# Decoder layer on one core: causal masks and results of the attention spread over other engines

## The reference

```python
x = layernorm(x + linear_attention(x))          # 16 heads of 64, relu features
x = layernorm(x + xattn(x, ctx))                # below
x = layernorm(x + ffn(x))                       # 8 experts, each row goes to one

# xattn: 16 heads of 16
att  = einsum('bhqd,bhkd->bhqk', q, k) * scale
att  = where(causal, att, -inf)
y    = einsum('bhqk,bhkd->bhqd', softmax(att), v)
attc = einsum('bhqd,bhkd->bhqk', qc, kc) * scale    # 1024 context rows, no mask
y    = y + einsum('bhqk,bhkd->bhqd', softmax(attc), vc)
return y @ Wp + bp
```

## Time and profile before

| what | value |
|---|---|
| median of 3 runs | 2330.27 us (2329.63 to 2338.28) |
| the profiled execution | 2329.88 us |
| its span | 2328.1 us |
| granted TensorE clock, mean | 0.993 |
| TensorE busy | 96% |
| VectorE busy | 60% |
| ScalarE busy | 45% |
| POOL busy | 13% |
| mean DMA rate | 101 GB/s |

### The profile page before, as it was taken

One profiled execution on the slowest core, in us unless ns is written; L12 is line 12 of the kernel. 1 busy time (PEld: TensorE's weight loads), 2 busy tenths in 40 slices (PEclk: granted clock), 3 DMA queues, 4 the chain that ended last, 5 costly groups with the idle time before them and its releaser, 6 DMA issues. The chain is left out here.

```text
span 2328.1 us, 52307 instructions
## 1 busy us (share of the span) xinstructions
PE 2229.4 (96%) x17506; PEld 1405.5 (60%) x17507; DVE 1401.9 (60%) x3568; ACT 1046.8 (45%) x1432; POOL 309.6 (13%) x516
## 2 busy tenths in 40 slices
PE   8999999999999999999999999999999999799998
PEld 4556555656465556555565656564655565499997
DVE  2578357844785458735883478447854686245554
ACT  1256524652466226632564256524662366233332
POOL 1010011101100110011010111011001101122222
PEclk9999999999999999999999999999999999899999
DMA  7440035102510162005300350026102520655553
GB/s 236 161 152 24 1 114 187 47 2 83 203 61 2 48 229 70 2 11 195 118 24 4 131 179 35 1 83 217 47 2 77 201 69 2 210 175 183 183 181 107
DMA packets 116585, 236.20 MB, mean 101 GB/s; under 512 B 19790, under 2 KB 43471, under 8 KB 114160
## 3 DMA queue, kind: packets, MB, share of 16 engines
q1 hardware_dynamic: 112928, 224.56, 28.8%
q0 software_dynamic: 3408, 8.41, 1.0%
HBM read 154.37 MB, written 73.17 MB: 98 GB/s over the span
## 5 line engine op out<-in xcount | busy, mean ns | idle before, releaser
L1152 ACT ACTIVATE es<-ps 128x1024 f32<-128x1024 f32 (+1 forms) x704 | 659.7, 983 | 306.7 <-PE ps L764 250.3
L1350 DVE TENSOR_REDUCE craw<-ps 128x1 f32<-128x512 f32 x1024 | 641.0, 683 | 131.8 <-PE ps L727 120.4
L727 PE MATMUL ps<-hk,hq 64*128 64x512 f32 x1024 | 279.2, 464 | 19.9 <-DVE craw L1350 12.0
L792 PE MATMUL ps<-es,vca 128*17 128x256 f32 x4096 | 276.7, 382 | 1.2 <-ACT es L1152 1.1
L1347 DVE TENSOR_REDUCE craw<-ps 128x1 f32<-128x512 f32 (+3 forms) x512 | 219.5, 484 | 75.8 <-PE ps L723 72.0
L762 PE MATMUL ps<-hq,hk 64*128 64x512 f32 x1024 | 235.5, 428 | 1.6 <-ACT es L1152 1.6
L727 PEld LDWEIGHTS ps<-hk,hq 64*128 64x128 f32 x1024 | 130.3, 184 | 176.6 <-DVE craw L1350 114.0
L632 POOL TENSOR_SCALAR_AFFINE_SELECT es<-es 128x256 f32<-128x256 f32 x256 | 99.4, 406 | 991.7 <-ACT es L1152 990.9
L764 PE MATMUL ps<-mrow,minus 64*128 64x512 f32 x1024 | 215.5, 391 | 0.0
L1661 ACT ACTIVATE hT<-ph,b1s 128x128 f32<-128x128 f32 x312 | 88.9, 368 | 183.9 <-PE ph L1624 183.9
L792 PEld LDWEIGHTS ps<-es,vca 128*17 128x17 f32 x4096 | 93.9, 96 | 115.1 <-issue 62.4
(11 more groups left out here) (206 smaller groups left out, 2812.4 us busy)
## 6 DMA issues: line engine op xcount, KB each, us to landing
w1s<-in_w1T SPq DMA_DIRECT2D x39, 1024.0 KB, 5.3
hk<-scr_kc SPq DMA_DIRECT2D x64, 512.0 KB, 5.2
scr_kc<-staged SPq DMA_DIRECT2D x16, 1024.0 KB, 4.3
scr_qc<-staged SPq DMA_DIRECT2D x32, 512.0 KB, 4.6
scr_q<-staged SPq DMA_DIRECT2D x32, 512.0 KB, 5.1
hq<-scr_qc SPq DMA_DIRECT2D x56, 256.0 KB, 5.0
hq<-scr_q SPq DMA_DIRECT2D x56, 256.0 KB, 4.2
hk<-scr_k SPq DMA_DIRECT2D x56, 256.0 KB, 5.2
```

The costliest lines, as they stand in the source:

```text
L727: last = mm(pb, hq[i][at, T + t * P:T + (t + 1) * P], hk[i][at, T + half * BANK:T + (half + 1) * BANK], start=True, stop=True)
L792: last = mm(z[row:row + VW, (2 - len(tiles)) * P:2 * P], (va if own else vca)[:, j, p * HB + a, :], weights, start=n in (0, NSELF), stop=n ...
L1152: nc.scalar.activation(es[:, k % ERING, :].rearrange("p (a c) -> p a c", a=HB)[:, :, 0:w], eslot[k % 2][:].rearrange("p (a c) -> p a c", a ...
L1350: last = v.reduce_max(craw[p % 2][:, t, a:a + 1, half], pb, AX.X)
```

## The change

- The two mask matmuls of each self tile go. VectorE takes the masked maximum in one operation, `tensor_tensor_reduce`: it adds `causal` (bf16, in SBUF, zeros with the mask as its last 128 columns) to the scores in PSUM, writes the sum back to the same place, and gives the maximum of each row. A semaphore increment on nothing (`s_held`) stands between the wait and this operation.
- `mpad` holds the maxima of all four query tiles in one 128x128 block, written by one operation. TensorE turns it with one transpose. ScalarE spreads it over `mrow` with four copies of 128 columns, each scaled by a column of `inblock` that is one on the partitions of its tile and zero elsewhere; `minus` has ones in more places to match.
- For the first seven pairs ScalarE copies the turned sums to `zt` in SBUF (`turned`), VectorE takes only the reciprocal, two maxima later in its order (DVE_ORDER, LATER), and POOL multiplies and adds (`results`). The bank of a turned result is freed by ScalarE. The last pair stays with VectorE.
- In the setup 12 DMAs become one (LOADS is 31, was 42). SP waits for the sums of the last pair ahead of the experts' weights.

```diff
+def reciprocals_later():
+    order = [e for e in ORDER if e[0] in ("max", "turn")]
+    for p in range(PAIRS - 1):
+        at = order.index(("turn", p, 0))
+        order.insert(min(at + 1 + LATER, order.index(("turn", p + 1, 0))), order[at])
+        del order[at]
+    return order
...
+        mpad = sb("mpad", [P, P])
+        zt = sb("zt", [P, 2 * NT * HB, VW])
...
             sp.wait_ge(s_av, NEXP * (nb + 1))
+            sp.wait_ge(s_ys, PAIRS * (nb + 1))
...
+                def results(p):
+                    pool.wait_ge(s_rec, b * (PAIRS - 1) + (p + 1))
+                    pool.sem_inc(s_past, 1)
+                    nc.gpsimd.tensor_tensor(yn[:], zt[:, :, 0:XD], rec[:].unsqueeze(2).broadcast_to([P, 2 * NT * HB, XD]),
+                                            ALU.mult).then_inc(s_yn, 1)
+                    pool.wait_ge(s_yn, b * (PAIRS - 1) + (p + 1))
+                    pool.sem_inc(s_past, 1)
+                    rows = sums_of()
+                    nc.gpsimd.tensor_tensor(y_s[:, :, p * HB * XD:(p + 1) * HB * XD], rows[:, 0], rows[:, 1],
+                                            ALU.add).then_inc(s_ys, 1)
...
                     if kind == "row":
                         pe.wait_ge(s_mrow, cur(b, PAIRS, p + 1))
+                    elif kind == "turn" and former != LAST_TURN:
+                        pe.wait_ge(s_zt, cur(b, PAIRS - 1, p + 1))
...
-                        mm(pb[:, col:col + w], hq[i][at, t * P:(t + 1) * P], hk[i][at, 0:w], start=True, stop=False)
-                        for half in range(2):
-                            last = mm(pb[:, col + w - P:col + w], iden2[at, half, :], mqk2[at, half, :],
-                                      start=False, stop=half == 1)
+                        last = mm(pb[:, col:col + w], hq[i][at, t * P:(t + 1) * P], hk[i][at, 0:w], start=True, stop=True)
...
-                for t in range(NT):
-                    last = tr(pb[:, t * P:(t + 1) * P], mpad[:, t, :], ident[:])
-                last.then_inc(s_ring, 1)
+                tr(pb[:, 0:P], mpad[:], ident[:]).then_inc(s_ring, 1)
...
-                    nc.scalar.activation(mrow[p % 2][:], mbank[n % MBANKS], ACT.Copy).then_inc(s_mrow, 1)
+                    for t in range(NT):
+                        last = nc.scalar.activation(mrow[p % 2][:, t * P:(t + 1) * P], mbank[n % MBANKS][:, 0:P],
+                                                    ACT.Copy, scale=inblock[:, t:t + 1])
+                    last.then_inc(s_mrow, 1)
...
+                def turned(p):
+                    s = RING_AT["turn", p, 0]
+                    act.wait_ge(s_ring, cur(b, NRING, s + 1))
+                    act.wait_ge(s_ys, cur(b, PAIRS, p))
+                    tv = mbank[s % MBANKS].rearrange("p (n d) -> p n d", d=ZW)
+                    nc.scalar.activation(zt[:], tv[:, :, 0:VW], ACT.Copy).then_inc(s_zt, 1)
...
                     if n >= 2 * NT:
+                        dve.sem_inc(s_held, 1)
                         for t, col in MAX_SELF[n - 2 * NT]:
-                            last = v.reduce_max(craw[p % 2][:, t, a:a + 1, 2], pb[:, col:col + (t + 1) * P], AX.X)
+                            own = pb[:, col:col + (t + 1) * P]
+                            last = v.tensor_tensor_reduce(own, own, causal[:, (NT - 1 - t) * P:NT * P], 1.0, LOWEST,
+                                                          ALU.add, ALU.max, craw[p % 2][:, t, a:a + 1, 0])
...
-                        v.tensor_copy(rows[:, :, :, 0], raw[2])
-                        v.tensor_tensor(rows[:, :, :, 1], raw[0], raw[1], ALU.max).then_inc(s_max, 1)
+                        rows = mpad[:].rearrange("p (a t c) -> p t a c", a=HB, t=NT)
+                        v.tensor_tensor(rows[:, :, :, 0:2], craw[p % 2][:, :, :, 0:2], craw[p % 2][:, :, :, 0:3:2],
+                                        ALU.max).then_inc(s_max, 1)
+
+                def reciprocals(p):
+
+                    dve.wait_ge(s_zt, cur(b, PAIRS - 1, p + 1))
+                    v.reciprocal(rec[:], zt[:, :, XD]).then_inc(s_rec, 1)
```

More of the change, by code:

```diff
@@ L39 @@
 NEG = -1e30
+LOWEST = -3.0e38
 HROW = 4 * XD
+MROW = HROW // NT
 ZW = 32
@@ L102 @@
 BEHIND = 4
+LATER = 2
 SWAP = (0, 1)
@@ L165 @@
 ORDER = heads_order()
+def reciprocals_later():
[5 more added lines that the diff above has]
+    return order
+DVE_ORDER = reciprocals_later()
 RING = [e for e in ORDER if e[0] in ("max", "row", "turn")]
 RING_AT = {e: n for n, e in enumerate(RING)}
-NRING, NRED = len(RING), sum(e[0] != "row" for e in RING)
-RED_AT = {e: sum(f[0] != "row" for f in RING[:n + 1]) for n, e in enumerate(RING)}
+NRING, NRED = len(RING), sum(e[0] == "max" for e in RING) + 1
+LAST_TURN = ("turn", PAIRS - 1, 0)
+RED_AT = {e: sum(f[0] == "max" or f == LAST_TURN for f in RING[:n + 1]) for n, e in enumerate(RING)}
 NEXP = PAIRS * NU
@@ L435, in _ @@
             const(number[:], number_d)
-            for n, src in enumerate((ident_d, mask_qk, mask_kq)):
-                for half in range(2):
-                    for at in range(2):
-                        const(cstage[at * HROW:(at + 1) * HROW, n, half, :], src[half * HROW:(half + 1) * HROW])
+            const(r_s[:, 0, 0:P], mask_qk)
             const(wvl[:], wv_l.rearrange("(k p) r -> p k r", p=P))
@@ L623, in _, with cut @@
                                             stage[:, stg, 0, at:at + T].bitcast(F32), ALU.subtract).then_inc(s_low, 1)
[L625 to L634, removed]
+                def cut(p, n):
+                    k = p * NU + n
+                    pool.wait_ge(s_exp, cur(b, NEXP, k + 1))
+                    pool.sem_inc(s_past, 1)
+                    for j, col in EXP_SELF[n]:
+                        block = es[:, k % ERING, :].rearrange("p (a c) -> p a c", a=HB)[:, :, col:col + P]
+                        last = nc.gpsimd.affine_select(block, block, [[0, HB], [1, P]], ALU.is_ge, 0.0, base=0,
+                                                       channel_multiplier=-1)
+                    last.then_inc(s_cut, 1)
+                def results(p):
[4 more added lines that the diff above has]
+                    pool.wait_ge(s_yn, b * (PAIRS - 1) + (p + 1))
+                    pool.sem_inc(s_past, 1)
+                    rows = sums_of()
+                    nc.gpsimd.tensor_tensor(y_s[:, :, p * HB * XD:(p + 1) * HB * XD], rows[:, 0], rows[:, 1],
+                                            ALU.add).then_inc(s_ys, 1)
+                for kind, p, n in ORDER:
+                    if kind == "exp" and n < NSELF:
+                        cut(p, n)
+                    elif kind == "turn" and p < PAIRS - 1:
+                        results(p)
                 pool.wait_ge(s_act, cur(b, N_ACT, ACT_AT["kf1"]))
@@ L1165, in _ @@
                         maxima_rows(p)
+                    elif kind == "turn" and p < PAIRS - 1:
+                        turned(p)
                     elif kind == "exp":
@@ L1355, in reduce, with last_results @@
                             dve.wait_ge(s_ring, cur(b, NRING, RING_AT["row", p - 1, 0] + 1))
-                        raw = [craw[p % 2][:, :, :, w] for w in range(3)]
-                        rows = mpad[:].rearrange("p t (a c) -> p t a c", a=HB)
-                        v.tensor_copy(rows[:, :, :, 0], raw[2])
-                        v.tensor_tensor(rows[:, :, :, 1], raw[0], raw[1], ALU.max).then_inc(s_max, 1)
-                def results(p):
+                        rows = mpad[:].rearrange("p (a t c) -> p t a c", a=HB, t=NT)
[4 more added lines that the diff above has]
+                    v.reciprocal(rec[:], zt[:, :, XD]).then_inc(s_rec, 1)
+                def last_results():
+                    p = PAIRS - 1
                     s = RING_AT["turn", p, 0]
+                    dve.wait_ge(s_ys, cur(b, PAIRS, p))
                     dve.wait_ge(s_ring, cur(b, NRING, s + 1))
@@ L1369, in results @@
                     dve.wait_ge(s_red, cur(b, NRED, RED_AT["turn", p, 0]))
-                    rows = yn[:].rearrange("p (w t a) d -> p w t (a d)", w=2, t=NT)
+                    rows = sums_of()
                     v.tensor_tensor(y_s[:, :, p * HB * XD:(p + 1) * HB * XD], rows[:, 0], rows[:, 1], ALU.add).then_inc(s_ys, 1)
                     dve.wait_ge(s_ys, cur(b, PAIRS, p + 1))
-                for kind, p, n in ORDER:
+                for kind, p, n in DVE_ORDER:
                     if kind == "max":
                         reduce(p, n)
+                    elif kind == "turn" and p == PAIRS - 1:
+                        last_results()
                     elif kind == "turn":
-                        results(p)
+                        reciprocals(p)
                 dve.wait_ge(s_xb, cur(b, 2, 2))
```

32 lines of the change are left out of this document (19 added, 13 removed).

## The result

The changed kernel takes 2303.03 us (median of 4 runs, 2301.82 to 2304.03) against 2329.95 us before on the same chip: a ratio of 0.9878, 95% interval [0.9866, 0.989]. The forecast was 2304.0. The profiled execution took 2301.82 us, its span is 2299.9, and its mean granted clock is 0.989 where before it was 0.993. That last number is the first hint that the agreement hides something.

A forecast was written before the change was run, and what follows sets the result against it. The prediction took TensorE and VectorE, both nearly full and joined by three banks of scores, as the bound; 3.2 us a sequence times 8 gave 26 us, and 2329.9 - 26 = 2304 us, range 2263 to 2348.

The forecast's parts named there:

- the walk: Step-by-step timing of TensorE and VectorE through one sequence's sections: 3.2 us gained a sequence, times 8, 26 us in all.
- Masked maximum: On VectorE, the new operation with two outputs: 0.11 us over the plain reduction, bounds 0.00 and 0.23 us.
- cheap mask: Rival: masked maximum under 0.05 us over the reduction, VectorE saving up to 0.88 us a pair more; 2270 us, chance 0.24.
- dear mask: Rival: masked maximum at 0.23 us over the reduction, VectorE's extra time counting whole; slower, 2358 us, chance 0.21.
- First pattern: Sections where an earlier pair's results stand between VectorE's masked maxima: 8.1 us instead of 8.86, gain 0.9, three a sequence.
- Second pattern: Sections where the results stand ahead of VectorE's masked maxima: 0.3 us lost, given back by the shorter turn; gain 0.
- First pair's maxima: Maxima between feature products at a sequence's first pair: roughly 0.5 us gained a sequence.
- Last row: Behind a sequence's last row, the shorter turn of the maxima and ScalarE's longer row cancel.
- Covers: Idle time on ScalarE hides its added copies: no cost while it lasts, without it 0.6 us in the pairs concerned.
- ScalarE pays: Rival: the four row copies delay the exponentials behind them and TensorE waits for a score bank; 2328 us, chance 0.06.
- Nothing surfaces: Rival: three banks of scores turn all of TensorE's relief into waits; 2330 us, chance 0.04.
- signs named: Expected in the profile: VectorE's busy time within 20 us, its waits for TensorE down, TensorE's waits for VectorE up.

The follow-up runs named there:

- row_later: The changed kernel with the last pair's row moved behind two further exponentials, one entry of the order: 2281.67 us.
- rl_dose: row_later with one more small VectorE copy, read by nothing, behind each masked maximum of pairs 1 to 7: 2311.15 us.
- masks_back: The changed kernel with the mask matmuls back on TensorE and plain maxima on VectorE: 2316.93 us.
- fill: The changed kernel with five unused products of 512 columns on TensorE ahead of the last pair's turn of the maxima: 2298.54 us.
- results_back: The changed kernel with the results of all pairs back on VectorE between the maxima: 2310.69 us.
- only_masks: The kernel before with the masked maxima on VectorE alone; transposes, copy and results stay as before: 2328.70 us.
- only_results: The kernel before with only the results of seven pairs moved to ScalarE and POOL: 2328.00 us.
- turn_back: The changed kernel with four transposes and one ScalarE copy for a pair's maxima again: 2309.20 us.

## Why the prediction was right

The sum was right to 1 us, and that was luck in part: a sequence gained 1.3 us more than forecast between its first and last row, and gave back about as much behind the last.

**Where the gain comes from: wrong.** "Its work doesn't fall; the gain is what it idles on TensorE today." It was the other way round: VectorE's busy time fell by 29.0 us, about the whole gain, and what it idles stayed the same, 926 us of the span before (2328.1 - 1401.9) and 927 after, with 192.4 us of waits for scores in both. The sum came out all the same because it was built from the walk, and not from this sentence.

**Masked maximum: mis-sized.** "I take 0.03 + 0.08 = 0.11" over the reduction. Two of 512 columns take 1.35 us (638.08 to 638.70 + 0.73), where two reductions take 1.29; the six smaller ones take 2.31 (640.10 to 642.11 + 0.47, less 0.17 for the reciprocal between them), where the reductions took 2.12. That is 0.03 each, in both. The first term was right. The second, a price of 0.08 for the second output, was wrong: that instruction exists, 141 ns long, and runs beside its neighbour, so that two follow each other by 0.62 us where 0.73 was forecast. What does cost comes behind a wait: the first masked maximum starts 0.69 us behind its first product (637.39), where the forecast took the reduction's 0.54. By its own bounds this was the rival *cheap mask*.

**What VectorE saves in a masked section.** For that rival I wrote "TensorE, then the bound, keeps about a third". With 8 x 0.08 = 0.64 us a pair saved over the forecast, of which two thirds count, that gives 2304 - 24 = 2280. It is near row_later's 2281.67, but row_later also moves the last row, so this proves no third. What rl_dose does show is the rule for the *dear mask*, "it counts whole", for all that delays the row: 0.24 to 0.63 us of delay surfaced as 0.25 to 0.61. The whole saving would then be 36 us; between the rows only some 10 us over the forecast came, and the two patterns show why. A mask as dear as 0.23 us would by the same rule have made the kernel slower, as that rival said; no run had one.

**First pattern: right, by errors that offset.** 8.1 us forecast, 7.99 measured. The third tile starts 2.02 us behind the first, 1.79 forecast: it waits for TensorE, which comes 0.2 later than in the walk, and not for VectorE. From there to the first context maximum it is 2.77 us instead of 3.18, the cheap mask. From there to the resumption it is 3.20 instead of 3.12, because the turn is shorter by 0.33 us (0.26 us from the turn to the weighing, 0.59 before), and not by the 0.42 that the forecast took.

**Second pattern: wrong.** "Gain 0." It gained 0.58 us. The forecast let the section grow by 0.3 because the mask was dear; at 0.03 it doesn't. Pair 1's section gained 0.7, those of pairs 3 and 5 0.6 each, which is 1.9 in a sequence beside 2.6 in the three of the first pattern; the steps from a second pattern to the next first one, "unchanged" in the forecast, take back 0.16 each. From first row to last the timeline gives 4.0 where the forecast had 2.7.

**First pair's maxima: right.** 0.66 us gained (ScalarE's copy of the first row of a sequence stands at 70.09 us from its start, before at 70.75), 0.5 forecast.

**Last row: a term was missing.** "Behind the last row the shorter turn and ScalarE's longer row cancel." These two do: from the turn of the last row on TensorE to the copy to `yT_s` it takes 25.13 us in before, and 25.17 to 25.20 in masks_back and in the sequences without a fall of fill and results_back, which all have one turn and four copies. In after it takes 26.2. The 1.1 us more, some 9 in eight, are the fall of the clock. Within one kernel, a sequence with a fall behind the last row takes 1.0 to 1.6 us more than one without. Beside it the wait ahead of that row grew from 1.21 to 1.45 us. row_later, which fills the wait, removes the fall and most of the wait. I had looked at the granted clock only where the engines are busiest. The trace of before had no fall there to show; its one fall, among the first pair's maxima, made that sequence 247.63 us long.

**The parts need each other.** On row_later they are worth 24.5, 16.5 and 11.7 us, 52.7 in all; the whole change there is worth 37.8. The difference has to be read with care: undone alone, a part also spoils what the others gave. Put on before alone, the masks bring 1.3 us, which the interval does not tell from nothing, and the results 2.0. My sum charged the results' 1.0 us to VectorE's total, as an offset to the masks'; it is that, and masked maxima behind the results also start 0.27 to 0.64 us late, as only_masks shows. The masked maximum alone was, on this kernel, worth nothing.

**Covers.** *ScalarE pays* did not come about: its copy takes 0.40 us (0.45 forecast), the row 1.14 (1.2), and POOL's product and sum are 0.62 and 0.46 us, waited for by nothing on the path. (The 107.3 us that VectorE's reciprocal waits for ScalarE's copy are eight waits behind the last maximum of a sequence, where VectorE has nothing else to do.) *Nothing surfaces* is excluded by the time. The start moved by up to 2.1 us between the kernels of this study (the loop begins 54.6 to 56.7 us in), with no order in the edits that I can see; the periods leave it out. Of the signs named, TensorE's waits for VectorE did go up, from 114.0 to 126.5 us; VectorE's busy time was to stay within 20 us and its waits for TensorE to go down, and neither did. One bound in the list of rivals doesn't follow from its rule: a mask at 0.05 us gives 2304 - 27 = 2277 if the saving counts whole and 2286 at two thirds, and not 2282.

**What stays open.** What makes the clock fall was not settled. The wait's length goes with it, but does not decide:

| kernel | idle ahead of the last row, us | sequences with a fall behind it |
|---|---|---|
| before | 1.21 | 0 of 8 |
| masks_back | 1.14 | 0 of 8 |
| only_results | 1.14 | 1 of 8 |
| after | 1.45 | 8 of 8 |
| results_back | 1.45 | 6 of 8 |
| only_masks | 1.45 | 6 of 8 |
| turn_back | 1.44 | 2 of 8 |
| fill | 0.38, then five products | 4 of 8 |
| row_later | 0.51 | 0 of 8 |

What the 0.64 us behind the sum in only_masks consists of was not tried. Nor was a dose on VectorE that stays clear of POOL; at pair 1's 0.24 us a pair it would have cost some 13 us, an estimate from 0.24 x 56.

The version that beats both is row_later: 2281.67 us, 48.3 under before and 21.4 under the change.

## What to carry to other kernels

Two engines that hand a few banks to each other can both show idle time and have no slack: put a small operation that nothing reads on one of them and see whether it surfaces. Here all of it did that delayed the row, and only the part ahead of one short wait was hidden. Look at how long each of the added operations takes, too; 72 of 448 ran into POOL's and took three times as long. Price a change at its edges: where a pipeline drains, a wait that grew by 0.24 us came with a fall of TensorE's clock that cost about 1 us in each sequence, and moving one entry of the order was then worth 21.4 us beside the whole change's 26.9. And undo each part of a bundle on a base without such a disturbance; on the disturbed one the prices were lower by 4 to 11 us.

## What the runs showed of the hardware

- The second instruction of an operation that writes its accumulator (141 ns) adds no time that can be seen between two such operations: at 512 columns one costs 0.03 us more than a plain reduction.
- The masked maximum starts 0.69 us behind the first product it waits for, the plain reduction 0.54. Behind a sum on VectorE itself it started 0.64 us after the sum's end in one section of a sequence and 0.27 in two; a plain reduction, 0.12.
- TensorE's granted clock fell to 1.2 GHz for 3.4 us behind an idle 1.45 us in each of 8 sequences of after; behind the same 1.44 us in turn_back in 2 of 8; and behind five products that followed an idle 0.38 us in 4 of 8 (fill).
- A small VectorE copy of 0.17 us puts the next operation 0.07 us later. The 72 copies of rl_dose that started while POOL ran a product or a sum took 0.48 us on the average and ended 0.03 us behind POOL's operation; the 376 others took 0.16.
